# Preparing the second feed-forward's weights during the first layer, and separate stacks for batch 0's first heads

## The reference, cut to what matters

```
x = x + tanh(g_xattn[0]) * sigmoid_attention(layernorm(x), ctx, ctx)
x = x + tanh(g_ffn[0])   * routed_ffn(layernorm(x))          # top 256 of 512 tokens, GELU, w1 512x2048, w2 2048x512
x = x + tanh(g_xattn[1]) * w8a8_attention(layernorm(x), ctx, mask)   # 16 heads of 32
x = x + tanh(g_ffn[1])   * bitlinear_ffn(layernorm(x))       # silu, W1 2048x512, W2 512x2048

# bitlinear:
def _weight_quant(w):
    scale = 1.0 / jnp.clip(jnp.mean(jnp.abs(w)), 1e-05)
    wq = jnp.clip(jnp.round(w * scale), -1.0, 1.0) / scale
```

## Time and profile before

| what | us |
|---|---|
| median of 3 runs (1026.59 to 1028.52) | 1027.84 |
| the profiled execution | 1027.91 |
| its span, first to last instruction | 1026.1 |
| TensorE busy | 899.2 (88%) |
| VectorE busy | 699.0 (68%) |
| ScalarE busy | 540.0 (53%) |
| POOL busy | 71.5 (7%) |
| mean granted TensorE clock, share of full | 0.959 |

### The profile page before, as it was taken

One profiled execution on the slowest core, in us unless ns is written; L12 is line 12 of the kernel. 1 busy time (PEld: TensorE's weight loads), 2 busy tenths in 40 slices (PEclk: granted clock), 3 DMA queues, 4 the chain that ended last, 5 costly groups with the idle time before them and its releaser, 6 DMA issues.

```text
span 1026.1 us, 15751 instructions
## 1 busy us (share of the span) xinstructions
PE 899.2 (88%) x5584; PEld 589.6 (57%) x5592; DVE 699.0 (68%) x1890; ACT 540.0 (53%) x1072; POOL 71.5 (7%) x73
## 2 busy tenths in 40 slices
PE   3989999999997973799898899898899898899567
PEld 2878767676774642566444576443566444567233
DVE  5995872424220684799786799786799787899564
ACT  4546211111110672689446689456688547688243
POOL 2000222121200000000100000100000010000100
PEclk9989999999999987899999999998999999999779
DMA  6435642121200958600179300178200179200001
GB/s 196 141 135 164 210 150 72 56 69 55 70 1 21 353 162 159 165 4 2 42 157 174 116 7 1 43 152 179 88 34 2 42 141 188 83 1 2 1 1 42
DMA packets 49581, 94.43 MB, mean 92 GB/s; under 512 B 8284, under 2 KB 8284, under 8 KB 48480
## 3 DMA queue, kind: packets, MB, share of 16 engines
q1 hardware_dynamic: 43584, 82.37, 30.1%
q0 software_dynamic: 3136, 10.52, 3.0%
q10 hardware_dynamic: 2784, 0.54, 0.4%
HBM read 47.23 MB, written 14.75 MB: 60 GB/s over the span
## 4 chain that ended last, share of the span: by engine, by line
PE 35%; DVE 10%; SPq 7%; issue 6%; ACT 5%; DMA 4%; POOL 0%; POOLq 0%; DVEq 0%; ACTq 0%
PE psum L1390 7%; PE psum L1407 6%; PE psum L1365 6%; SPq L1041 6%; PE psum L1463 5%; PE psum L1433 5%; DMA k<-k_lo 4%; ACT probs L1191 2%; PE psum L1332 1%; PE psum L1449 1%; DVE amax L1612 1%; SPq L1052 1%; DVE xn L1780 1%; PE psum L1416 1%; DVE stats L1775 1%
## 5 line engine op out<-in xcount | busy, mean ns | idle before, releaser
L1191 ACT ACTIVATE probs<-psum,neg_max 128x512 f32<-128x512 f32 x256 | 175.0, 693 | 32.3 <-DVE neg_max L1674 32.1
L1674 DVE CUSTOM_DVE_ANT_0 psum<-psum,m_in 128x512 f32<-128x512 f32 x256 | 174.0, 703 | 18.1 <-issue 18.1
L1390 PE MATMUL psum<-ident,probs 128*128 128x128 f32 x1024 | 153.8, 274 | 0.0
L1390 PEld LDWEIGHTS psum<-ident,probs 128*128 128x128 f32 x1024 | 127.3, 141 | 20.5 <-issue 3.3
L1365 PE MATMUL psum<-k,q 128*128 128x512 f32 x256 | 125.6, 496 | 13.6 <-ACT probs L1191 7.9
L568 PE MATMUL psum<-w_sb,hT 128*128 128x512 f32 x256 | 114.4, 592 | 0.0
L465 ACT ACTIVATE hT<-psum,b_col 128x256 f32<-128x256 f32 x64 | 26.9, 471 | 153.6 <-PE psum L490 153.5
L1700 DVE COPY probsT<-psum 128x512 f32<-128x512 f32 x128 | 87.7, 686 | 2.8 <-PE psum L1390 2.5
L1182 ACT COPY probsT<-psum 128x512 f32<-128x512 f32 x128 | 75.2, 588 | 19.3 <-PE psum L1390 19.3
L488 PE MATMUL psum<-xselT_hi,w_hi 128*128 128x256 f32 x256 | 81.6, 319 | 1.6 <-ACT xselT_hi L459 1.6
L1365 PEld LDWEIGHTS psum<-k,q 128*128 128x128 f32 x256 | 48.9, 191 | 50.0 <-ACT probs L1191 32.9
(11 more groups left out here) (212 smaller groups left out, 1541.6 us busy)
## 6 DMA issues: line engine op xcount, KB each, us to landing
c_in<-in_ctx_dram SPq DMA_DIRECT2D x8, 1024.0 KB, 5.6
bw_in<-in_L_ffn_W_dram SPq DMA_DIRECT2D x8, 1024.0 KB, 12.3
...
q<-q_hi SPq DMA_DIRECT2D x64, 128.0 KB, 3.5
q<-q_lo SPq DMA_DIRECT2D x64, 128.0 KB, 3.5
xres<-in_x_dram SPq DMA_DIRECT2D x4, 1024.0 KB, 6.3
w_raw<-in_L_ffn_w_dram POOLq DMA_DIRECT2D x4, 1024.0 KB, 5.5
```

What stands on the lines that cost most here:

```text
L1191: act.activation(probs[:, u % 4, :], psum[u % SCORE_BANKS][:, :], ACT.Exp, scale=-1.0, bias=neg_max[:, u:u + 1], accum_out=prob_sum[:, nt, ...
L1390: mm = pe.transpose(turn_bank(u)[:, l * P:(l + 1) * P], probs[:, u % 4, l * P:(l + 1) * P], ident[:, :])
L1674: dve.tensor_tensor_reduce(bank[:, :], bank[:, :], m_in[:, nt, :], -1.0, LOWEST, ALU.add, ALU.min, neg_max[:, u:u + 1]).then_inc(masked_re ...
```

## The change

The preparation of W1 and W2 moves into layer 0's feed-forward, where it runs on ScalarE, TensorE and a little VectorE, one piece for each slot. A single buffer `bw_raw` takes a chunk; ScalarE itself issues each load, after its last use of the buffer, and so every chunk is loaded twice, once for its magnitudes and once for rounding. Slots 1 to 8 take one magnitude each (the absolute values are written back in place), slots 11 to 28 round a chunk, make it whole and turn its two halves through one PSUM bank. The sums over partitions are made in slots 9 and 11 and taken up by VectorE during batch 1. To make room, xres holds three batches instead of four (x of batch 3 waits for batch 0's stored rows), and x_sel, score_row, rank_a, the attention weights and their loads change places.

In layer 1 the whole preparation is gone. Batch 0's key and query parts of tile 0 lie in a place of their own (`first_parts`, where probs will be), the others apart from each other, so that no part waits for a stack. SP stacks tile 0 of the keys (16 DMAs of 64 KB), then tiles 1 to 3 (16 of 192 KB), then tiles 2 and 3 of the queries (16 of 128 KB); POOL stacks tiles 0 and 1 of the queries, 16 DMAs of 64 KB each. The first scores wait only for tile 0 of both, unit 16 for tile 1 and all keys, unit 32 for the rest. The residual moves from steps 8 to 11 to steps 24 to 27, in every batch, because in batch 0 its place holds query parts.

Cut to its core:

```diff
-        xres = sb("xres", [P, B, T, C])
+        xres = sb("xres", [P, 3, T, C])
...
+        bw_raw = at("bw_raw", [P, BWC], F32, sig_at + 8 * K)
+        bw_whole = at("bw_whole", [P, BWC], BF16, ctxT_at + 8 * K)
...
+                    if b == B - 2:
+                        sp.wait_ge(xnr_ready, T)
+                        sp.wait_ge(x1_stored, 16)
                     sp.wait_ge(xn_lo_ready, b * T + T)
-                    sp.dma_start(xres[:, b + 1, :, :], rows(x, b + 1)).then_inc(x_loaded, 16)
+                    sp.dma_start(xres[:, (b + 1) % 3, :, :], rows(x, b + 1)).then_inc(x_loaded, 16)
...
-                    sp.wait_ge(xnr_ready, T * (b + 1))
+                    sp.wait_ge(xn_sel_stored, 16 * T * (b + 1))
...
+                next_inputs(0)
+                next_inputs(1)
+                store_x1(0)
+                next_inputs(2)
+                store_x1(1)
...
+                def load_chunk(n):
+                    i, k = divmod(n % 8, 4)
+                    dst, src = chunk(i, k)
+                    act.dma_start(dst, src).then_inc(bw_loaded, 16)
+
+                def magnitude(n):
+
+                    act.wait_ge(bw_loaded, 16 * (n + 1))
+                    act.activation(bw_raw[:, :], bw_raw[:, :], ACT.Abs,
+                                   accum_out=bw_part[:, n // 4, n % 4:n % 4 + 1]).then_inc(magnitude_ready, 1)
+                    act.wait_ge(magnitude_ready, n + 1)
+                    load_chunk(n + 1)
+
+                def round_chunk(m):
+
+                    act.wait_ge(bw_loaded, 16 * (m + 9))
+                    act.wait_ge(bw_inv_ready, m // 4 + 1)
+                    act.activation(bw_raw[:, :], bw_raw[:, :], ACT.Identity, scale=bw_inv[:, m // 4:m // 4 + 1],
+                                   bias=round_cols[:, 0:1]).then_inc(bw_rounding, 1)
+
+                def whole_chunk(m):
+
+                    act.wait_ge(bw_rounding, m + 1)
+                    if m:
+                        act.wait_ge(bwT_psum, 2 * m)
+                    act.activation(bw_whole[:, :], bw_raw[:, :], ACT.Identity,
+                                   bias=round_cols[:, 1:2]).then_inc(bw_whole_ready, 1)
+                    if m + 1 < 8:
+                        act.wait_ge(bw_whole_ready, m + 1)
+                        load_chunk(m + 9)
+
+                def turned_chunk(m, half):
+
+                    act.wait_ge(bwT_psum, 2 * m + half + 1)
+                    act.activation(bwT_half(m // 4, 2 * (m % 4) + half),
+                                   psum_b[7].rearrange("p (a b) -> p a b", a=(2, 8)[m // 4]), ACT.Sign,
+                                   saturate=False).then_inc(bwT_ready, 1)
+
+                def weights(slot):
+
+                    if slot == 0:
+                        act.wait_ge(round_ready, 2)
+                        load_chunk(0)
+                    if 1 <= slot <= 8:
+                        magnitude(slot - 1)
+                    m, second = divmod(slot - FIRST_TURN, 2)
+                    if 0 <= m < 8:
+                        if second:
+                            whole_chunk(m)
+                        else:
+                            if m:
+                                turned_chunk(m - 1, 0)
+                            round_chunk(m)
+                    if 1 <= m <= 8:
+                        if second:
+                            turned_chunk(m - 1, 1)
+                        elif m == 8:
+                            turned_chunk(m - 1, 0)
...
+                        if pair < PAIRS - 1 or b + 1 == B:
+                            weights(b * PAIRS + pair)
                     if b + 1 < B:
                         selected_highs(b + 1)
+                        weights(b * PAIRS + PAIRS - 1)
                         gelu(b + 1, 0)
+                        weights((b + 1) * PAIRS)
...
+                def bw_sums(i):
+
+                    pe.wait_ge(magnitude_ready, 4 * i + 4)
+                    pe.matmul(psum[5 + i][:, 0:4], ones[:, :], bw_part[:, i, :], start=True, stop=True).then_inc(bw_sum_psum, 1)
+
+                def turn_chunk(m, half):
+
+                    pe.wait_ge(bw_whole_ready, m + 1)
+                    if 2 * m + half:
+                        pe.wait_ge(bwT_ready, 2 * m + half)
...
+                        mm = pe.transpose(psum_b[7][:, j * P:(j + 1) * P], bw_whole[:, o:o + P], ident_b[:, :])
+                    mm.then_inc(bwT_psum, 1)
+
+                def weights(slot):
+
+                    if slot in (9, 11):
+                        bw_sums((slot - 9) // 2)
+                    m, half = divmod(slot - FIRST_TURN - 2, 2)
+                    if 0 <= m < 8:
+                        turn_chunk(m, half)
...
                         if b + 1 < B and pair == PAIRS - 1:
+                            if b == 1:
+                                pe.wait_ge(bw_inv_ready, 2)
                             turn_selected(b + 1)
+                        weights(b * PAIRS + pair)
                         down(b, pair - 1)
                         if b + 1 < B and pair == 3:
+                        weights((b + 1) * PAIRS)
...
+                def bw_unit(i):
...
+                    dve.wait_ge(bw_sum_psum, i + 1)
+                    link(dve.tensor_reduce(bw_sum[:, i:i + 1], psum[5 + i][:, 0:4], AX.X, ALU.add))
...
                         scores(link, b + 1)
+                        if b == 1:
+                            bw_unit(0)
                         ranks(link, b + 1)
                         assert link.count == CHAIN_B
+                        if b == 1:
+                            bw_unit(1)
...
+        first_parts = at("first_parts", [P, 4, S], F32R, probs_at)
+        k_hi_rest = at("k_hi_rest", [P, CT_ - 1, S], F32R, arena)
+        k_lo_rest = at("k_lo_rest", [P, CT_ - 1, S], F32R, arena + 6 * K)
+        q_hi_rest = at("q_hi_rest", [P, CT_ - 1, S], F32R, xres_at)
+        q_lo_one = at("q_lo_one", [P, S], F32R, xres_at + 6 * K)
+        q_lo_rest = at("q_lo_rest", [P, 2, S], F32R, arena + 12 * K)
+        k_hi0 = [first_parts[:, 0, :]] + [k_hi_rest[:, c, :] for c in range(CT_ - 1)]
+        k_lo0 = [first_parts[:, 1, :]] + [k_lo_rest[:, c, :] for c in range(CT_ - 1)]
+        q_hi0 = [first_parts[:, 2, :]] + [q_hi_rest[:, c, :] for c in range(CT_ - 1)]
+        q_lo0 = [first_parts[:, 3, :], q_lo_one[:, :]] + [q_lo_rest[:, c, :] for c in range(2)]
...
+        RESIDUAL_STEP = 24
...
+                for c, stacked in enumerate(first_q_stacked):
+                    pool.wait_ge(q_hi_ready, c + 1)
+                    pool.wait_ge(q_lo_ready, c + 1)
+                    for g, part in enumerate((q_hi0, q_hi0, q_lo0, q_lo0)):
+                        for r in range(HPG):
+                            pool.dma_start(q4[HD * g:HD * (g + 1), c * HPG + r, :].bitcast(F32),
+                                           part[c][HD * r:HD * (r + 1), :].bitcast(F32)).then_inc(stacked, 16)
...
-                sp.wait_ge(bw_whole_ready, 4)
-                stack_keys(0)
-                sp.wait_ge(bw_whole_ready, 8)
-                stack_queries(0, q_hi0, q_lo0)
+                sp.wait_ge(k_hi_ready, 1)
+                sp.wait_ge(k_lo_ready, 1)
+                for g, part in enumerate((k_hi0, k_lo0, k_hi0, k_lo0)):
+                    for r in range(HPG):
+                        sp.dma_start(k4[HD * g:HD * (g + 1), r, :].bitcast(F32),
+                                     part[0][HD * r:HD * (r + 1), :].bitcast(F32)).then_inc(first_k_stacked, 16)
+                sp.wait_ge(k_hi_ready, CT_)
+                sp.wait_ge(k_lo_ready, CT_)
+                for g, part in enumerate((k_hi_rest, k_lo_rest, k_hi_rest, k_lo_rest)):
+                    for r in range(HPG):
+                        sp.dma_start(k4[HD * g:HD * (g + 1), HPG + r::HPG, :].bitcast(F32),
+                                     part[HD * r:HD * (r + 1), :, :].bitcast(F32)).then_inc(k_stacked, 16)
+                sp.wait_ge(q_hi_ready, CT_)
+                sp.wait_ge(q_lo_ready, CT_)
+                q_hi_last = q_hi_rest[:, 1:CT_ - 1, :]
+                for g, part in enumerate((q_hi_last, q_hi_last, q_lo_rest, q_lo_rest)):
+                    for r in range(HPG):
+                        sp.dma_start(q4[HD * g:HD * (g + 1), 2 * HPG + r::HPG, :].bitcast(F32),
+                                     part[HD * r:HD * (r + 1), :, :].bitcast(F32)).then_inc(q_stacked[1], 16)
...
-                round_chunk(0, 1)
-                round_chunk(0, 3)
-                for k in range(3):
-                    magnitude(1, k)
-                turned_bw(0)
                 act.wait_ge(bq_ready, 1)
-                round_chunk(1, 1)
-                round_chunk(1, 3)
-                act.wait_ge(k_stacked, 16 * STACKS)
                 query_highs(0, q_hi0)
-                turned_bw(1)
...
+                    if b == 0:
+                        pe.wait_ge(first_k_stacked, 16 * STACKS)
+                        pe.wait_ge(first_q_stacked[0], 16 * STACKS)
```

(35 more changed lines are left out.)

236 lines of the change are left out of this document (88 added, 148 removed).

## The result

The changed kernel took 1016.46 us (median of 7 runs, 1014.7 to 1021.66) against 1027.68 us (7 runs, 1025.61 to 1028.52) of the kernel before: ratio 0.9899, 95% interval 0.9879 to 0.9919. The forecast was 1021.3 us, faster. The span of the profiled execution fell by 11.4 us, from 1026.1 to 1014.7.

A forecast was written before the change was run, and what follows sets the result against it. TensorE bounds layer 0's feed-forward; the stretch to layer 1's first score waits on stacking, with DMA queues full meanwhile. 1027.9 + 19.1 (layer 0) - 25.7 (start of layer 1) = 1021.3 us, range 1009 to 1036.

The forecast's parts named there:

- TensorE's 9.0 and 0.5 us: Layer 0's feed-forward: 128 transposes cost TensorE 9.0 us and the two sums' small matmuls 0.5 us, all exposed.
- The wait for the GELUs, 4.5 us in slot 7: Layer 0: TensorE waits 3.7 us for slot 7's GELU, plus 0.8 for the wq load and selected tokens.
- The clock, 2.9 us: Layer 0: after the wait in slot 7, TensorE runs at half clock for 5.8 us, costing 2.9 us more.
- Bank 7, 2.2 us: Layer 0, slots 11 to 28: turned halves come about 1.1 us late where slots lie 2.8 us apart; 2.2 us.
- The rule on loads: Layer 0: skill's fit gives 4.4 us per 1 MB load; 7.4 us of wait and clock vanish, total about 1014.
- The first score, 25.7 us: Start of layer 1: first score moves from 416.6 to 390.9 us, with POOL's pace 0.84 us and landing 3.5.
- The keys are no limit: Start of layer 1: the keys' stacking DMAs are done near 382 us, before the first score at 390.9.
- Rival D: Start of layer 1: tile 0's queries queue behind the keys' megabytes, landing near 399; total 1029.4, no change; chance 0.08.
- A: Layer 0: ScalarE's loads take 7.6 us, a round 9.7; layer 0 costs 33.3, total 1035.5, slower; chance 0.17.
- B: Layer 1 start: POOL pace 1.58 us, gain 8.4, total 1038.6, chance 0.15; VectorE locking out descriptors, total 1026.8, chance 0.06.
- C: Loads of 5.0 us or late stall, POOL at 0.54: layer 0 costs 11.7, gain 30.2, total 1009.4, chance 0.17.
- Units 8 and 16: Layer 1 attention: unit 16's tile 1 queries land 404.3, needed 410.0; tiles 2 and 3 near 395, unit 8 about 404.

## Why the prediction was right, and where not

Direction, time and range held, and both big terms were right to within 3 us. That they were so close is in part luck: inside each of them errors of 1 to 5 us cancelled, and the 2.4 us behind the first score stood in no term. Of the signs that the prediction gave, the end of layer 0, and no wait at units 8 and 16, held; one wait near 171 us and a pace of 0.84 us did not, and two signs of being wrong came true, several waits in slots 4 to 9 and loads of over 6 us (4 of the 16).

**TensorE's 9.0 and 0.5 us.** Busy 9.9 and 0.6; doubled, 7.0 more, so "all of it exposed" is shown. The prediction had no row for the 1.0 us of the 16 groups nor for the sums' 0.5; they came out near.

**The wait for the GELUs, 4.5 us in slot 7.** Mechanism right and shown by spreading the magnitudes: rounds longer than a slot, GELU of slot k behind magnitude k - 2. In place and shape it was off. It came as 1.24, 2.83 and 1.49 us in slots 5, 6 and 7, 5.6 in sum. Two values were wrong: the first load landed at 136.96 us, not 134.5 (it took 10.3 us in the stores' and w2's company, though it was issued at 126.64, before the GELU), and the rounds took 6.7 to 7.8 us, but one took 10.3, for which I had allowed only 0.8 (wq and the selected tokens beside it).

**The clock, 2.9 us.** 1.7 us. Three short waits do not do what one long one does: the clock fell behind the 2.83 only. It was so in all seven profiles with the magnitudes in slots 1 to 8 and wq's load in its old place: the wait in slot 6 was 2.5 to 3.6 us and half clock followed, those in slots 5 and 7 were 0.5 to 1.8 us and the clock stayed full. But behind 3.24 us in slot 7, with wq late, it did not fall at all (3.70 for the eight matmuls). So the earlier trace rows was a fair bound, not a price. **Bank 7, 2.2 us:** 2.0, in two waits, as forecast.

**The rule on loads.** Landings of these 1 MB loads were 4.6 us at best, 5.3 in the median and 10.3 at worst. The Trainium skill, "DMA: Bandwidth & Descriptors", section "Anatomy of one DMA", has a fit measured on DMAs that POOL issues, which gives an estimate of 4.4 us for 1 MB. ScalarE issued these, and not one was as fast. By 4.4 us no GELU would have been late; three were late, so the rows were the better guide to the waits. The total of about 1014 us that went with the fit is nearer to the measured one, 2.5 us off for 4.8, but by luck: it leaves out 7.3 us of waits and clock that are there, and the surplus of 2.9 us in layer 1 and 2.4 us behind it happen to make up for most of that. I had also read the earlier trace rows too kindly. It does not say "alone", and its worst load took 15.2 us: wv's, issued among w2's loads, which is the company that the first chunk's load had.

**The first score, 25.7 us.** Measured 28.6. The start was 1.3 us earlier than forecast. The pace was mis-sized: 0.49 us, under my lower bound of 0.54, for 0.84; the 0.30 us that stands ahead of an indirect DMA is not there between these plain ones. That is 5.2 us too much. The landing was mis-sized the other way, 7.0 for 3.5: the 3.5 of the earlier trace rows is a median over all batches. 1.3 + 5.2 - 3.5 leaves 3.0, the surplus.

**"The keys are no limit."** This is the step of the mechanism that failed. I let the keys be through near 382 us of before's clock, 48 us behind the first transpose, and that was 3 us too early (the last was issued 43.0 us behind it, at 396.36, and took 8.4 us to land, 51.4 us behind it). But I priced the queries, which start at 40 us, as if nothing were beside them, neither these keys nor the 2 MB of queries that SP sends next. Rival D named this; it happened in part and cost 5 us of the gain (54.3 against 49.2 with the keys held), not 8. Its argument against, that POOL's queue is another than SP's, did not help: the two queues together moved 234 GB/s from 393.05 to 407.50 us, and tile 0's queries had to take their share of it.

**Rivals.** A: the loads were between my value and its: median 5.3, once 10.3; the waits came to 5.6 us, half of what would have made the kernel slower. B: POOL's pace excludes it. Of its second half (the Trainium skill, "SBUF — State Buffer", section "SBUF: two separate sides") nothing is seen. Tile 1's issues took 0.50 us each; in the changed kernel VectorE had little to do beside them (busy for 1.0 of 7.9 us), but with the other keys held it was busy for 5.6 of the 6.4 us from 401.5 to 407.9, masking scores in PSUM and copying out of it, and they still took 0.50 us. So this work of VectorE does not hold them up; a copy from SBUF to SBUF, which is the case that the Trainium skill describes there, stood beside them in no run here. C: POOL's half of it came true. **Units 8 and 16** did not wait, as forecast; but unit 8 is the next bound, as holding the keys and the lows first both show. **After the first score** nothing changed beyond the spread of single executions.
